# Products of B and input in groups of four tiles, with B rows loaded in each half

## The chip, the core and the metric

The kernel runs on one core of a Trainium2 chip. TensorE (PE) multiplies matrices, VectorE (DVE), ScalarE (ACT) and GpSimd (POOL) work on tiles of 128 partitions, and SyncE (SP) issues transfers between HBM and the on-chip memory. Each engine runs its own list of instructions in order; semaphores tie the lists together. The metric is the device time of one execution in microseconds.

## The reference

The input is 8 batch rows of 512 steps with 128 channels. Four layers with residuals follow each other: a selective state-space layer (S6), a mixture of experts, a diagonal state-space layer (S5), and the same experts again. The part that the change touches is S6, with 256 inner channels and 64 states:

```python
def step(h, t):
    delta_t, B_t, x_t, C_t = t
    dA = jnp.exp(delta_t[..., None] * A)
    dB = delta_t[..., None] * B_t[:, None, :]
    h = dA * h + dB * x_t[..., None]
    y_t = C_t * jnp.sum(h, axis=-1)
    return (h, y_t)
...
x = x + _L0_attn_a_ref(_layernorm(x, axis=-1), ...)
x = x + _L0_ffn_ref(_layernorm(x, axis=-1), ...)
x = x + _L0_attn_b_ref(_layernorm(x, axis=-1), ...)
x = x + _L0_ffn_ref(_layernorm(x, axis=-1), ...)
```

So for each batch row there are 256 x 64 state sequences of 512 steps. Each obeys h = dA * h + w, where w is the product of u = delta * x (one value per channel and step) and B (one value per state and step). The experts (8 of them, all computed and weighted with the routing's weights) and S5 are dense products with short elementwise work between.

## The kernel before

One batch row is one turn of the pipeline, `scan(Turn(...))`; turns count from 0 to 7. A turn has 128 slots, and slot k holds tile k of the scan: 128 partitions (32 groups of channels by 4 groups of states) by 512 steps. `tile_of(k)` gives the half of the channels (k // 64), the state row n (0 to 15) and the channel q (0 to 3) within a group of four. Two tiles make a pair, called a duo in the code.

For each tile ScalarE computes the decay `da` (line 736, an exponential, into PSUM), GpSimd the product `w` = `ur` times `br` (line 845, two tiles in one instruction), VectorE the scan `h` (line 1146), and TensorE sums `h` over states into `ys` (line 569), four tiles at a time. Buffers form rings: `da` holds 4 tiles, `w` 6 tiles (`W_RING` of 3 pairs), `h` 8 tiles. ScalarE and GpSimd therefore run ahead of VectorE by at most 4 and 6 tiles. The pair that may reuse a buffer of `w` is found by `before_in_ring`, which begins anew in every turn: pair 0 takes buffer 0, which pair 63 of the turn before used.

`ur` (input rows u spread over the partitions, two halves of 64 tiles) and `dr` (step rows delta) are loaded from scratch tensors in HBM, where the previous turn stored them. `br` holds all 16 rows of B per partition group; both halves read them. It is loaded once per turn in four chunks of four rows, 1 MB each (line 352, `load_b`), in the turn before and at the start of the turn.

Between the tiles each engine does the other layers' work, at slots that a written table fixes. `weave(pair, tasks)` calls `pair(slot)` and then every task whose slot has come; this is the order in the engine's list, and no engine can pass an instruction that waits. `pre_a` is the preparation of the next batch row (projections, softplus, stores, from slot 64 on), `post` the later layers of the previous row, `late` the last part of the experts of the row before that. GpSimd's tasks are:

- `expert_sums` (line 789): adds the weighted outputs `yk` of an expert to x. It waits for ScalarE (line 697). It stands at slots 6, 13, 18, 24 and 29 (late), 43, 47, 54, 58, 65, 69, 76 and 80 (first experts), 120, 124 and behind 127 (second experts).
- `rstd` (lines 751 to 757): four small instructions of a layer normalization, at slots 13, 22, 70, 83 and 103. ScalarE's normalization and VectorE's statistics (`moments`, line 995) stand on either side.
- `gates` (lines 820 and 823): products for the output gate, at slots 47, 48, 50 and 51, and a residual (line 828) at 54.
- lines 795, 798, 801 and 777: further products of whole rows, at slots 13, 17 and 106 to 107.

VectorE's statistics of the first experts' output stand at slot 77 and wait for the sum of the last expert, which GpSimd has at slot 80. In turn 0 there are no expert tasks at all, and in turn 1 no late ones.

## Time and profile before

| | |
|---|---|
| median of 3 runs | 1941.29 us (1937.05 to 1941.82) |
| span of the profiled execution | 1936.6 us |
| time of the profiled execution around its span | the page gives none |
| VectorE busy | 1522.2 us (79%) |
| GpSimd busy | 1516.6 us (78%) |
| TensorE busy (matmul) | 1377.6 us (71%) |
| ScalarE busy | 1294.2 us (67%) |
| moved by DMA | 88.34 MB, mean 46 GB/s |

The span goes from the first to the last instruction of one execution. Busy time is counted per engine, so the engines' figures do not add up to the span. In the rows further down, "idle before" is the time in which the engine stood still before an instruction, and the arrow names the engine and line whose semaphore came last; "issue" stands where the profile shows no releaser for the wait.

### The profile page before, as it was taken

Reading aid. Unit: us, or ns where it says so; the run is one execution under the profiler, and the core shown is the slowest. Engines: PE = TensorE matmul, PEld = TensorE weight load, DVE = VectorE, ACT = ScalarE, POOL = GpSimd, SP = SyncE. Lnnn points to the kernel's source line nnn. Section 1 sums busy time; section 2 is a strip of 40 time slices with the busy share of each in tenths; the row PEclk is TensorE's granted clock in tenths of the full one; section 3 lists DMA queues with packets and bytes.
Section 4 is the critical chain, followed back from the end, with each engine's and each line's share of the span. In section 5 each row is a group of like instructions: output and inputs, shape, how many; then the busy total and the mean of one; then the engine's idle time right before and its main releaser. Section 6 shows DMA issues by size and latency. Waiting matters only on the chain. (4 is left out here: it accounts for less than half of the span.)

```text
span 1936.6 us, 18983 instructions
## 1 busy us (share of the span) xinstructions
PE 1377.6 (71%) x5928; PEld 611.6 (32%) x5928; DVE 1522.2 (79%) x2109; ACT 1294.2 (67%) x2285; POOL 1516.6 (78%) x888
## 2 busy tenths in 40 slices
PE   3236458777885787768776778668787778668958
PEld 1001113224332343224332343224332343324535
DVE  3979887887888788897888888888878878895222
ACT  4447567677777777677777777777776867665423
POOL 0899899788897798877898798977998888974212
PEclk8557569889897989889898899889898898869969
DMA  3500500031001400031000400032000320000000
GB/s 102 195 0 25 184 1 1 25 109 71 12 1 31 173 12 1 25 109 71 12 1 25 169 11 11 1 103 102 11 1 25 109 71 6 1 6 1 6 1 6
DMA packets 34140, 88.34 MB, mean 46 GB/s; under 512 B 5363, under 2 KB 20598, under 8 KB 25846
## 3 DMA queue, kind: packets, MB, share of 16 engines
q1 hardware_dynamic: 32454, 87.12, 12.7%
q8 instruction: 47, 0.77, 0.2%
q14 instruction: 55, 0.45, 0.1%
q10 hardware_dynamic: 1584, 0.01, 0.0%
HBM read 75.58 MB, written 11.53 MB: 45 GB/s over the span
## 5 line engine op out<-in xcount | busy, mean ns | idle before, releaser
L1146 DVE TENSOR_TENSOR_SCAN h<-da,w 128x512 f32<-128x512 f32 x1024 | 1193.2, 1208 | 225.6 <-ACT da L736 127.5
L845 POOL TENSOR_TENSOR w<-ur,br 128x1024 f32<-128x1024 f32 x512 | 1197.1, 2362 | 158.5 <-DVE h L1146 146.3
L736 ACT ACTIVATE da<-dr,al 128x511 f32<-128x511 f32 x1024 | 683.4, 689 | 236.0 <-DVE h L1146 233.3
L569 PE MATMUL ys<-h,wsum 128*32 128x512 f32 x2048 | 331.8, 726 | 243.2 <-DVE h L1146 215.4
L502 PE MATMUL bankH<-nT,w 128*128 128x512 f32 x512 | 321.3, 713 | 99.8 <-DVE aq L1085 67.9
L789 POOL TENSOR_TENSOR x<-x,yk 128x512 f32<-128x512 f32 x128 | 163.2, 1275 | 193.2 <-ACT yk L697 175.2
L502 PE MATMUL bankG<-nT,w 128*128 128x512 f32 x512 | 292.8, 656 | 25.5 <-DVE aq L1085 25.5
L515 PEld LDWEIGHTS bankY<-w,aq 128*128 128x128 f32 x2048 | 259.2, 200 | 83.7 <-issue 74.1
L515 PE MATMUL bankY<-w,aq 128*128 128x128 f32 x2048 | 265.9, 286 | 9.7 <-DVE aq L1085 5.1
L697 ACT ACTIVATE yk<-bankY,rt 128x128 f32<-128x128 f32 x512 | 156.0, 365 | 132.7 <-PE bankY L515 112.3
L569 PEld LDWEIGHTS ys<-h,wsum 128*32 128x32 f32 x2048 | 43.6, 116 | 446.5 <-DVE h L1146 406.2
L502 PEld LDWEIGHTS bankH<-nT,w 128*128 128x128 f32 x512 | 89.1, 213 | 285.5 <-DVE aq L1085 115.0
L502 PEld LDWEIGHTS bankG<-nT,w 128*128 128x128 f32 x512 | 96.8, 209 | 183.9 <-DVE aq L1085 92.6
L1085 DVE TENSOR_TENSOR aq<-tq,bankH 128x512 f32<-128x512 f32 x64 | 42.8, 669 | 62.0 <-PE bankH L502 62.0
L736 ACT ACT_TABLE_LOAD x62 | 79.5, 1283 | 10.3 <-DMA dr<-d_rows 9.2
L472 PE MATMUL bankG<-xs,wx 128*128 128x512 f32 x64 | 43.7, 819 | 43.1 <-DVE sres L1013 42.3
L684 ACT ACT_TABLE_LOAD x55 | 70.6, 1283 | 1.0
L684 ACT ACTIVATE sq<-bankH 128x512 f32<-128x512 f32 x64 | 38.2, 597 | 46.2 <-PE bankH L502 46.2
L684 ACT ACTIVATE tq<-bankH 128x512 f32<-128x512 f32 x64 | 38.3, 599 | 32.4 <-PE bankH L502 32.1
L631 ACT ACTIVATE nrm<-x,nm,rs 128x128 f32<-128x128 f32 x96 | 39.4, 481 | 29.3 <-POOL nm L757 29.2
L1085 DVE TENSOR_TENSOR aq<-tq,bankG 128x512 f32<-128x512 f32 x64 | 42.6, 666 | 12.5 <-PE bankG L502 12.5
L684 ACT ACTIVATE sq<-bankG 128x512 f32<-128x512 f32 x64 | 38.2, 597 | 20.4 <-PE bankG L502 20.4
(178 smaller groups left out, 1040.4 us busy)
## 6 DMA issues: line engine op xcount, KB each, us to landing
br<-b_rows SPq DMA_DIRECT2D x32, 1024.0 KB, 11.7
dr<-d_rows SPq DMA_DIRECT2D x16, 1024.0 KB, 7.7
ur<-u_rows SPq DMA_DIRECT2D x16, 1024.0 KB, 7.5
d_rows<-vh SPq DMA_DIRECT2D x16, 256.0 KB
u_rows<-th SPq DMA_DIRECT2D x16, 256.0 KB
xnew<-in_L_attn_a_x_dram SPq DMA_DIRECT2D x8, 256.0 KB, 3.0
w<-in_L_ffn_W_dram SPq DMA_DIRECT2D x2, 1024.0 KB, 14.6
x<-in_L_attn_a_x_dram SPq DMA_DIRECT2D x8, 256.0 KB, 9.2
```

Source lines behind the costliest of these rows:

```text
L472: ins = nc.tensor.matmul(p[:, :], lhs(k), xs[:, k, :], start=(k == 0), stop=(k == 1))
L502: is_filled(t, f"{name}{m}_{n}", nc.tensor.matmul(p[:, :], wt[:, n // 2, n % 2 * 128:n % 2 * 128 + 128], nT[:, :], start=True, stop=True))
L515: ins = nc.tensor.matmul(p[:, a * 128:(a + 1) * 128], aq[:, (2 * n + k) % 4, a * 128:(a + 1) * 128], w3[:, n, k, :], start=(k == 0), stop= ...
L569: ins = nc.tensor.matmul(ys[32 * q:32 * q + 32, :], wsum[:, :], h[:, (2 * group + q // 2) % H_RING, q % 2, :], start=(n == 0), stop=(n == ...
L631: A(dst[:, a, :], src[:, a, :], ACT.Identity, bias=nm[:, k, a:a + 1], scale=rs[:, k, a:a + 1]).then_inc(normed[k], 1)
L684: A(zt[j % 4], p[:, :], ACT.Silu).then_inc(drained[BANK[f"h{m}_{j}"]], 1)
L697: ins = A(yk[:, a, :], p[:, a * 128:(a + 1) * 128], ACT.Copy, scale=rt[:, 0, a, e:e + 1])
L736: A(da[duo % D_RING][:, k % 2, 1:L], dr[:, half, q, 1:L], ACT.Exp, scale=nega[:, QUADS * half + q, n:n + 1]).then_inc(decay_ready, 1)
L789: G.tensor_tensor(total[:, :, :], total[:, :, :], yk[:, :, :], ALU.add).then_inc(added, 1)
L845: G.tensor_tensor(w[:, duo % W_RING, :, :], ur[:, half, q:q + 2, :], br[:, n:n + 1, :].to_broadcast([128, 2, L]), ALU.mult).then_inc(produ ...
L1085: drain(f"g{m}_{n}", V.tensor_tensor(aq[:, n % 4, :], zt[n % 4], p[:, :], ALU.mult))
L1146: V.tensor_tensor_scan(h[:, duo % H_RING, k % 2, :], da[duo % D_RING][:, k % 2, :], w[:, duo % W_RING, k % 2, :], 0.0, ALU.mult, ALU.add). ...
```

## The change

- GpSimd multiplies four tiles in one instruction: all four channels q of one state row n, at slots 0, 4, 8 and so on. 256 instructions of 128x2048 replace 512 of 128x1024.
- The ring `w` holds three such groups, twelve tiles, and is indexed by a count that runs on over the turns. `before_in_ring` is gone. A group waits for the scans of the group three before it. `h` is indexed by a running count as well.
- `br` shrinks to two chunks of four rows. Each chunk is loaded anew for each half: 8 chunks per turn, 64 loads of 1 MB instead of 32. A chunk's load waits until the chunk two before it has been multiplied, and is issued by SyncE when its list reaches slots 0, 16, 32 and so on.
- VectorE waits for a product once per four tiles instead of once per two.

```diff
-CHUNKS, PER_CHUNK = 4, 4
+CHUNKS, PER_CHUNK, B_RING = 8, 4, 2
+PER_LOAD = PAIRS // CHUNKS
...
-        w = sb("w", [128, W_RING, 2, L]); h = sb("h", [128, H_RING, 2, L])
+        w = sb("w", [128, W_RING, QUADS, L]); h = sb("h", [128, H_RING, 2, L])
...
+                i, n0 = chunk // CHUNKS, chunk % CHUNKS * PER_CHUNK % PER_QUAD
                 sp.wait_ge(b_stored, 16 * i + 16)
-                if not known(i, 1):
-                    sp.wait_ge(product_ready, DUOS * (i - 1) + DUO_HALF + 2 * PER_CHUNK * (chunk + 1))
...
+                if not known(chunk, B_RING):
+                    sp.wait_ge(product_ready, PER_CHUNK * (chunk - B_RING + 1))
...
             def scan(t):
                 def pair(k):
+                    if k % PER_LOAD == 0 and not (k == 0 and known(t.b, 1)) and (t.pre or k < PAIRS - PER_LOAD):
+                        load_b(CHUNKS * t.b + k // PER_LOAD + 1)
                     if k == 0 and not known(t.b, 1):
-                        load_b(t.b, CHUNKS - 1)
                         load_steps(t.b, 1)
...
-                    if k % 2:
+                    if k % QUADS:
                         return
...
-                    freed = before_in_ring(duo, W_RING)
-                    if not known(DUOS * t.b + freed, 0):
-                        pool.wait_ge(scanned, PAIRS * t.b + 2 * freed + 2)
-                    G.tensor_tensor(w[:, duo % W_RING, :, :], ur[:, half, q:q + 2, :],
-                                            br[:, n:n + 1, :].to_broadcast([128, 2, L]), ALU.mult).then_inc(product_ready, 1)
+                    chunk, quad = (PAIRS * t.b + k) // PER_LOAD, DUO_HALF * t.b + k // QUADS
+                    if k % PER_LOAD == 0:
+                        pool.wait_ge(b_in[chunk % B_RING], 16 * (chunk // B_RING) + 16)
+                    if not known(quad, W_RING):
+                        pool.wait_ge(scanned, QUADS * (quad - W_RING) + QUADS)
+                    row = n % PER_CHUNK
+                    G.tensor_tensor(w[:, quad % W_RING, :, :], ur[:, half, :, :],
+                                    br[:, chunk % B_RING, row:row + 1, :].to_broadcast([128, QUADS, L]), ALU.mult).then_inc(product_ready, 1)
...
+                    quad = DUO_HALF * t.b + k // QUADS
+                    if k % QUADS == 0:
+                        v.wait_ge(product_ready, quad + 1)
                     if k % 2 == 0:
-                        v.wait_ge(product_ready, DUOS * t.b + duo + 1)
```

GpSimd's list from slot 44 to slot 64, before (w is the product, x the expert sum, cg, xd and resa the gates and the residual):

```order
L845 TENSOR_TENSOR w<-ur,br 128x1024 [waits scanned] x2
L820 TENSOR_TENSOR cg<-cm,sres 128x512 [waits c_ready,ys_taken]
L789 TENSOR_TENSOR x<-x,yk 128x512 [waits added,drainedY,weighted]
L845 TENSOR_TENSOR w<-ur,br 128x1024 [waits scanned,b_in3]
L823 TENSOR_TENSOR xd<-xd,sres 128x512 [waits skip_ready]
L845 TENSOR_TENSOR w<-ur,br 128x1024 [waits scanned]
L820 TENSOR_TENSOR cg<-cm,sres 128x512
L823 TENSOR_TENSOR xd<-xd,sres 128x512 [waits skip_ready]
L845 TENSOR_TENSOR w<-ur,br 128x1024 [waits scanned] x2
L828 TENSOR_TENSOR resa<-xn,bcs 128x512 [waits normed0,x1_ready]
L789 TENSOR_TENSOR x<-x,yk 128x512 [waits added,drainedY,weighted]
```

The same place now:

```order
L842 TENSOR_TENSOR w<-ur,br 128x2048 [waits scanned]
L817 TENSOR_TENSOR cg<-cm,sres 128x512 [waits c_ready,ys_taken]
L786 TENSOR_TENSOR x<-x,yk 128x512 [waits added,drainedY,weighted]
L842 TENSOR_TENSOR w<-ur,br 128x2048 [waits scanned,b_in1]
L820 TENSOR_TENSOR xd<-xd,sres 128x512 [waits skip_ready]
L817 TENSOR_TENSOR cg<-cm,sres 128x512
L820 TENSOR_TENSOR xd<-xd,sres 128x512 [waits skip_ready]
L842 TENSOR_TENSOR w<-ur,br 128x2048 [waits scanned]
L825 TENSOR_TENSOR resa<-xn,bcs 128x512 [waits normed0,x1_ready]
L786 TENSOR_TENSOR x<-x,yk 128x512 [waits added,drainedY,weighted]
```

The products of tiles 50 and 51 have moved ahead of the gates at slots 48, 50 and 51.

GpSimd's list around a turn's start (slot 116 to slot 7), before; b_in0 and input_in0 mark the product of tile 0:

```order
L845 TENSOR_TENSOR w<-ur,br 128x1024 [waits scanned] x7
L789 TENSOR_TENSOR x<-x,yk 128x512 [waits drainedY,weighted]
L845 TENSOR_TENSOR w<-ur,br 128x1024 [waits scanned] x2
L789 TENSOR_TENSOR x<-x,yk 128x512 [waits added,drainedY,weighted]
L845 TENSOR_TENSOR w<-ur,br 128x1024 [waits scanned]
L789 TENSOR_TENSOR x<-x,yk 128x512 [waits added,drainedY,weighted]
L845 TENSOR_TENSOR w<-ur,br 128x1024 [waits scanned,b_in0,input_in0]
```

And now:

```order
L842 TENSOR_TENSOR w<-ur,br 128x2048 [waits scanned] x2
L786 TENSOR_TENSOR x<-x,yk 128x512 [waits drainedY,weighted]
L842 TENSOR_TENSOR w<-ur,br 128x2048 [waits scanned]
L786 TENSOR_TENSOR x<-x,yk 128x512 [waits added,drainedY,weighted] x2
L842 TENSOR_TENSOR w<-ur,br 128x2048 [waits scanned,b_in0,input_in0]
```

The last products of a turn (tiles 126 and 127) have moved ahead of the sum at slot 124, and two sums now stand directly in front of tile 0.

SyncE's list for the end of one turn and the start of the next, before (br is the load of B rows, dr and ur those of step and input rows, d_rows and u_rows the stores):

```order
L352 DMA br<-b_rows 128x1x2048 [waits product_ready,b_stored]
L319 DMA d_rows<-vh 4x32x512 [waits drainedG]
L325 DMA u_rows<-th 4x32x512 [waits inputs_ready]
L330 DMA dr<-d_rows 128x1x2048 [waits decay_ready,steps_stored0]
L330 DMA ur<-u_rows 128x1x2048 [waits product_ready,inputs_stored0]
L319 DMA d_rows<-vh 4x32x512 [waits drainedH]
L325 DMA u_rows<-th 4x32x512 [waits inputs_ready]
L352 DMA br<-b_rows 128x1x2048 [waits product_ready,b_stored] x3
L330 DMA dr<-d_rows 128x1x2048 [waits decay_ready,steps_stored1]
L330 DMA ur<-u_rows 128x1x2048 [waits product_ready,inputs_stored1]
```

And now:

```order
L349 DMA br<-b_rows 128x1x2048 [waits product_ready,b_stored]
L315 DMA d_rows<-vh 4x32x512 [waits drainedG]
L321 DMA u_rows<-th 4x32x512 [waits inputs_ready]
L326 DMA dr<-d_rows 128x1x2048 [waits decay_ready,steps_stored0]
L326 DMA ur<-u_rows 128x1x2048 [waits product_ready,inputs_stored0]
L315 DMA d_rows<-vh 4x32x512 [waits drainedH]
L321 DMA u_rows<-th 4x32x512 [waits inputs_ready]
L349 DMA br<-b_rows 128x1x2048 [waits product_ready,b_stored] x2
L326 DMA dr<-d_rows 128x1x2048 [waits decay_ready,steps_stored1]
L326 DMA ur<-u_rows 128x1x2048 [waits product_ready,inputs_stored1]
```

The load of a turn's first B chunk stood in the first of these rows and now stands in the eighth, behind both stores and both loads; the first row is now the last chunk of the running turn.

## Rows read from the trace of the kernel before

**Rows 1.** Costliest groups: line, engine, out<-in, shapes, count | busy us, mean ns | idle before us.

```profile
L845 POOL TENSOR_TENSOR w<-ur,br 128x1024 f32<-128x1024 f32 x512 | 1197.1, 2362 | 158.5 <-DVE h L1146 146.3
```

**Rows 2.** Waits: engine and line, what it waited for: us in total, times, longest.

```profile
POOL x L789 <- ACT yk L697: 175.2, 53, 17.5
POOL w L845 <- DVE h L1146: 146.3, 102, 5.9
DVE h L1146 <- issue: 52.9, 26, 3.0
DVE h L1146 <- POOL w L845: 3.2, 1, 3.2
```

**Rows 3.** Windows: stretch, us, busy us (and instructions) of PE, PEld, DVE, ACT, POOL; clock, DMA.

```profile
114.00:145.00 31.00, 7.82 (x36) 0.89 (x40) 19.48 (x18) 11.43 (x18) 31.00 (x18) 0.50 0.00 0
...
830.00:1040.00 210.00, 160.38 (x714) 73.17 (x713) 176.16 (x239) 155.64 (x275) 181.97 (x108) 0.88 0.13 45
```

**Rows 4.** Timeline, GpSimd at turn 4's start: start us, length, instruction xcount [idle before <-releaser].

```profile
884.22 1.27 POOL L789 TENSOR_TENSOR x<-x,yk 128x512 f32<-128x512 f32 x1 [1.37 <-ACT yk L697]
887.77 9.30 POOL L845 TENSOR_TENSOR w<-ur,br 128x1024 f32<-128x1024 f32 x4 [2.28 <-DVE h L1146]
```

**Rows 5.** Timeline, VectorE, turn 4's start (tiles 127 and 0) and tile 26.

```profile
886.38 1.22 DVE L1146 TENSOR_TENSOR_SCAN h<-da,w 128x512 f32<-128x512 f32 x1
890.22 2.34 DVE L1146 TENSOR_TENSOR_SCAN h<-da,w 128x512 f32<-128x512 f32 x2 [2.62 <-issue]
...
936.90 4.65 DVE L1146 TENSOR_TENSOR_SCAN h<-da,w 128x512 f32<-128x512 f32 x4 [1.20 <-issue]
```

**Rows 6.** Timeline, GpSimd, turn 4, from the sum before tile 48 to tile 61.

```profile
969.29 1.27 POOL L789 TENSOR_TENSOR x<-x,yk 128x512 f32<-128x512 f32 x1 [2.44 <-DVE h L1146]
970.51 2.36 POOL L845 TENSOR_TENSOR w<-ur,br 128x1024 f32<-128x1024 f32 x1
...
991.76 6.97 POOL L845 TENSOR_TENSOR w<-ur,br 128x1024 f32<-128x1024 f32 x3
```

**Rows 7.** Timeline, VectorE, the same stretch (first row: tiles 45 to 48; then 52, 56, 60).

```profile
969.73 4.56 DVE L1146 TENSOR_TENSOR_SCAN h<-da,w 128x512 f32<-128x512 f32 x4
...
981.27 3.54 DVE L1146 TENSOR_TENSOR_SCAN h<-da,w 128x512 f32<-128x512 f32 x3 [2.42 <-issue]
...
988.36 4.66 DVE L1146 TENSOR_TENSOR_SCAN h<-da,w 128x512 f32<-128x512 f32 x4 [1.26 <-issue]
...
994.21 1.22 DVE L1146 TENSOR_TENSOR_SCAN h<-da,w 128x512 f32<-128x512 f32 x1 [0.61 <-ACT da L736]
```

**Rows 8.** Timeline, GpSimd, turn 4, slots 69 to 80.

```profile
1006.82 1.27 POOL L789 TENSOR_TENSOR x<-x,yk 128x512 f32<-128x512 f32 x1 [2.25 <-ACT yk L697]
...
1010.35 0.20 POOL L751 TENSOR_TENSOR var<-bag,eps 128x4 f32<-128x4 f32 x1
...
1012.16 7.00 POOL L845 TENSOR_TENSOR w<-ur,br 128x1024 f32<-128x1024 f32 x3
...
1024.99 1.26 POOL L789 TENSOR_TENSOR x<-x,yk 128x512 f32<-128x512 f32 x1
```

**Rows 9.** Timeline, VectorE, turn 4, the statistics at slot 77.

```profile
1026.29 0.87 DVE L995 BATCH_NORM_STATS2 bst<-x 128x6 f32<-128x128 f32 x4 [2.08 <-POOL x L789]
```

**Rows 10.** Timeline, GpSimd, turn 0, tiles 6 to 47.

```profile
63.48 48.53 POOL L845 TENSOR_TENSOR w<-ur,br 128x1024 f32<-128x1024 f32 x21 [5.94 <-DVE h L1146]
```

**Rows 11.** Timeline, VectorE, turn 0 tile 71, turn 1 tiles 0 and 14.

```profile
155.81 4.57 DVE L1146 TENSOR_TENSOR_SCAN h<-da,w 128x512 f32<-128x512 f32 x4 [1.30 <-ACT da L736]
...
232.15 2.34 DVE L1146 TENSOR_TENSOR_SCAN h<-da,w 128x512 f32<-128x512 f32 x2 [2.61 <-issue]
...
251.35 3.53 DVE L1146 TENSOR_TENSOR_SCAN h<-da,w 128x512 f32<-128x512 f32 x3 [1.00 <-ACT da L736]
```

**Rows 12.** The tile br: from a DMA's issue to its landing.

```profile
DMA to landing us min/median/max: 4.8/11.7/15.7
```

More of the change, by code:

```diff
@@ L111, in tile_of @@
     return k // HALF, (k % HALF) // QUADS, k % QUADS
-def before_in_ring(duo, ring):
-    return duo - ring if duo >= ring else max(d for d in range(DUOS) if d % ring == duo % ring) - DUOS
 def moe_pe(m, late):
@@ L245, in hybrid_kernel @@
         delta_in = [sem("delta_in0"), sem("delta_in1")]; input_in = [sem("input_in0"), sem("input_in1")]
-        b_in = [sem(f"b_in{c}") for c in range(CHUNKS)]
+        b_in = [sem(f"b_in{c}") for c in range(B_RING)]
         decay_ready = sem("decay_ready"); product_ready = sem("product_ready")
@@ L363, in pre_a @@
                 store_b(t)
-                yield HALF + 18
-                load_b(i, 0)
+                if first:
+                    yield HALF + 18
+                    load_b(0)
                 yield SLOT["dt1"] + 10
@@ L374, in pre_a @@
                 store_inputs(t, 1)
-                for chunk in range(1, CHUNKS - 1):
-                    yield HALF + 18 + 16 * chunk
-                    load_b(i, chunk)
                 if first:
-                    load_b(i, CHUNKS - 1)
+                    yield HALF + 34
+                    load_b(1)
                     load_steps(i, 1)
@@ L568, in sum_states @@
                     for q in range(QUADS):
-                        ins = nc.tensor.matmul(ys[32 * q:32 * q + 32, :], wsum[:, :], h[:, (2 * group + q // 2) % H_RING, q % 2, :],
+                        ins = nc.tensor.matmul(ys[32 * q:32 * q + 32, :], wsum[:, :], h[:, (DUOS * t.b + 2 * group + q // 2) % H_RING, q % 2, :],
                                                start=(n == 0), stop=(n == PER_QUAD - 1))
@@ L831, in pair @@
                 def pair(k):
-                    if k % 2:
+                    if k % QUADS:
                         return
-                    half, n, q = tile_of(k)
-                    duo = k // 2
+                    half, n, _ = tile_of(k)
                     if k == 0 and known(t.b, 1):
```

19 lines of the change are left out of this document (9 added, 10 removed).

## The prediction

> **What bounds the kernel now.** Five views were read, in this order. The costliest groups of instructions show GpSimd's products of the reference's B and input term: 512 instructions of two tiles each, 2362 ns [rows 1]. A tile is one 128x512 piece of state, 128 of them in a turn (one batch row). The table of waits looks as if these products never mattered: VectorE's scans waited for them 3.2 us in all, and GpSimd waited 146.3 us for the scans and 175.2 us for ScalarE's weighted expert outputs [rows 2]. But 52.9 us of scan idle are put down to "issue", and the order of time explains that name: in one of the middle turns scans start at 890.22, 936.90, 981.27, 988.36 and 994.21, each after a gap [rows 5, 7], and the product they read ends about 0.1 us before. For the first, the product started at 887.77 and takes 2.36 us, so it ended at 890.13 [rows 4]. The windows say the same: from 114 to 145 us GpSimd was busy in all 31.00 us, VectorE in 19.48. In a middle window of 210 us neither is full, 182 and 176 us [rows 3]. So no engine bounds this kernel as a whole. The engines run written orders and hand the lateness round, and what decides is who is late at each place. I count five places per turn where GpSimd is: tile 0 (gap 2.62), 26 (1.20), 52 (2.42), 56 (1.26) and 60 (0.61), 8.1 us together [rows 5, 7]. In the first turn it is more. Turns are numbered from 0, so this one is turn 4.
>
> **What one product of four tiles costs.** No row shows a GpSimd instruction of 2048 columns. Starts tell more than lengths here: 21 two-tile products cover 48.53 us [rows 10], so (48.53 - 2.36)/20 = 2.31 us from one to the next, and the one-tile instruction at 969.29 is followed at 970.51, 1.22 us [rows 6]. A further tile costs 2.31 - 1.22 = 1.09, the fixed part is 0.13. Bounds: 4 x 1.09 = 4.36 with no fixed part at all, 4 x 1.22 = 4.88 with the whole of it each time. I take 1.22 + 3 x 1.09 = 4.49, nearest to both rows, against 4.62 for two of today's: 0.13 us saved per four tiles, 256 x 0.13 = 33 us of GpSimd over the run. Its end is seen 0.05 later (2.36 against 2.31).
> By the rows, a product's span is 2.36 us and its spacing 2.31. The Trainium skill (Perfetto Trace Analysis, section GPSIMD Engine Instruction) says that a span reported for GpSimd is not to be trusted and that starts of consecutive instructions should be used; the trace agrees, by 0.05 us. Going by spans one would have 2.36 + 2 x 1.09 = 4.54 and a saving of 0.18, or 46 us; on the path computed below this changes the time by under 3 us.
>
> **The ring.** The old ring held three pairs, six tiles, and began again in each turn: since 64 pairs are not a multiple of 3, pair 0 took the buffer of pair 63 and had to wait for the last scan. The new one holds twelve tiles and runs on across turns.
> At a middle turn's start: the last expert sum starts at 884.22 and ends GpSimd's work at 885.5; then it waits 2.28 us for the scan that ends at 887.60 [rows 4, 5]. Without that wait the four-tile product runs 885.45 to 889.99, and scan 0 can start at 890.1 instead of 890.22. The wait goes, and the longer instruction takes its place: gain 0.1 us, not 2.6. The sum itself cannot come earlier, since it waits for ScalarE, which follows the scans.
>
> **Tiles 24 to 31.** Before tile 14 GpSimd stood waiting for ScalarE (the sum behind tile 12, see the order); products 14 and 15 now fill that wait. From there to tile 29 eight products of 2.31 (18.5 us) become four of 4.49 (18.0), with the same small work between: the gap at tile 26 [rows 5] goes, a smaller one appears before tile 28, which waits for its whole four. I count 0.3 us gained.
>
> **Tiles 48 to 63: the place that costs.** The sum in front of product 48 starts at 969.29 whatever the ring [rows 6]; its row names a scan, but by the order it can only wait for ScalarE's outputs, which ScalarE gives in step with the scans. Today products of 48-49, 50-51 and so on follow with a gate instruction (1.22 us) between them, and scan 48 starts at 969.73 + 3 x 1.12 = 973.1 [rows 7]. After the change the first product is whole only at 970.51 + 4.54 = 975.05: scan 48 starts 2.0 us later. Then three gate instructions (3.66): second product from 978.66, whole at 983.2, scan 52 at 983.3 against 981.27, +2.0. Then two (2.44): scan 56 at 990.2 against 988.36, +1.8. Then one (1.22): scan 60 at 995.9 against 994.21, +1.7. GpSimd has no less to do before tile 63 than before, and the scans get nothing until four tiles are ready. With the 0.3 from above: +1.4 us at tile 60. All of the expert work behind (TensorE's products wait for VectorE's gating in between) moves with it.
>
> **Tiles 69 to 80.** The sum at 1006.82 waits for ScalarE [rows 8], so it moves by 1.4 too. From its start to the end of the last sum (1024.99 + 1.26 = 1026.25) it is 19.43 us today. After: sum 1.22, the four small normalization instructions 1.81 (1010.35 to 1012.16), two products 8.98, sum 1.22, product 4.49, sum 1.26 = 18.98. VectorE stands at exactly this end, 2.08 us until 1026.29 [rows 9]: it is later by 1.4 - 0.45 = 0.9 us. Behind it, products have 4 to 7 us to spare and nothing of GpSimd's decides until the next turn. So a middle turn becomes 0.9 us longer. Six of the eight (turns 2 to 7): +5.4 us.
>
> **First two turns.** Here no expert sums hold GpSimd back, and the ring's size works. It waited 5.94 us for a scan after three products [rows 10]; with twelve tiles allowed it arrives at the gates about 6.0 us earlier than at 112.0. Nine two-tile products up to tile 64 (20.8 us) become five of four (22.4): 1.6 back, so scan 64 comes 4.5 us earlier. The normalization behind it, for which the scans waited 1.30 us [rows 11], also comes earlier: 5.5. At the second turn's start the gap of 2.61 us goes fully, as no sum stands in front; with 0.7 of small gaps in the 20 tiles before, and the gap of 1.00 at tile 14 [rows 11], 4.3 more. Against that the second turn pays the 48 to 80 stretch, +0.9. Together -5.5 - 4.3 + 0.9 = -8.9 us.
>
> **B rows.** Each half reads them anew: 64 loads of 1 MB instead of 32, through SyncE's queue. A load lands in 11.7 us in the middle, 15.7 at worst [rows 12], and a chunk is four products, at least 4 x 4.49 = 18 us. It is asked for when the chunk before last is consumed, so one chunk of work covers it, and I cost it at nothing. The cover is thinnest for a turn's first chunk, behind two stores and two loads of 1 MB: in the first turn it should land about when it is needed. What waits behind a late B load on SyncE are the next turn's step and input rows, needed half a turn later. Without the cover each chunk would lose what it is late by.
>
> **Sum.** -8.9 + 5.4 = -3.5 us. The page gives the profiled execution's span, 1936.6 us, and no other time of it; the median of the runs is 1941.3, 4.7 above, which I take as what lies around it and the spread. Forecast 1941.3 - 3.5 = 1938 us. Unknown sizes: product 4.36 to 4.88 moves a middle turn by -0.8 to +2.3; early gain 5 to 11. That puts the likeliest case between 1932 and 1945.
>
> **Rivals.**
> *The twelve-tile lead works everywhere.* For it: GpSimd waited 146.3 us for scans [rows 2], all of it lead that it could not build. If the gaps at tiles 0 and 26 go in all turns (3.8 x 7 = 27 us, less 5 that I have counted already), the time is 1938 - 22 = 1916. Against it: the 175.2 us behind ScalarE cap the lead in front of tiles 0 and 48.
> *First tile late.* The slower end: the two extra tiles in front of scan 48 (+2.0) and in front of the sum at tile 80 are paid in full, as nothing is won back between tile 60 and 80. Price 2.0 x 7 = 14, early gain 5.5: 1941.3 + 8.5 = 1950. It decides from about 1.4 us per turn upward. For it: TensorE's and ScalarE's gaps at 64, 84 and 108 hang on scans too. Against: the sum of 18.98 against 19.43.
> *B late.* If the first chunk of each turn came 5 us late, 7 x 5 = 35: 1976. Against it: [rows 12].
> *No fixed part is saved.* Then four tiles cost 4.62, a middle turn +1.5: 1942.
>
> **Chances.** Forecast's own case 0.60, lead works 0.16, first tile late 0.18, B late 0.03, nothing saved 0.03. About 0.3%, 6 us, is what a measurement can tell from no change. Of the forecast's 0.60, 0.16 lie under 1935.5, 0.40 within, 0.04 above 1947. Faster 0.16 + 0.16 = 0.32; same 0.40 + 0.03 = 0.43; slower 0.04 + 0.18 + 0.03 = 0.25. The range leaves out the far half of the first rival and the last one: 1921 to 1951.
>
> **What would show it.** Products near 4.5 us, 256 of them. Scan 0 of turn 1 about 9 us earlier, later turns each 0.5 to 1.5 us longer than before; gaps of about 2 us before tiles 48, 52 and of 1.3 before 56; the wait in front of the sum-bound statistics at tile 77 still there. Waits of GpSimd's products for scans nearly gone, for ScalarE's outputs grown. A product that waits for a B load, or middle turns shorter than before, would prove me wrong.

## The result and the profile after

The kernel after took 1952.01 us (median of 4 runs, 1950.81 to 1955.07) against 1941.05 before: ratio 1.0066, 95% interval 1.0051 to 1.0080. It is slower, by 0.7%. The forecast was 1938, and the time lies just outside the range that ended at 1951. The profiled execution took 1950.81 us for a span of 1949.0, so 1.8 us lie around the span (I had taken 4.7 for it and the spread).

What was forecast of the instruction itself came. One row answers [rows 1]:

```profile
L842 POOL TENSOR_TENSOR w<-ur,br 128x2048 f32<-128x2048 f32 x256 | 1154.9, 4529 | 70.7 <-DVE h L1146 58.0 <-issue 12.6
```

256 products of 4.53 us, 4.48 from start to start (885.80, 9.00 us for two, below); GpSimd is busy 1478.2 us instead of 1516.6. The products' waits for scans fell from 146.3 to 58.0, and the expert sums' waits for ScalarE rose from 175.2 to 234.5 [rows 2]:

```profile
POOL x L786 <- ACT yk L694: 234.5, 60, 18.8
```

B rows are loaded 64 times, landing in 4.5 us at least, 5.0 median, 12.3 at most (before [rows 12]), and no product waited for one.

The turn's start, GpSimd and VectorE, against [rows 4, 5]: the product follows the last sum at once, and scan 0 is late as before.

```profile
884.57 1.26 POOL L786 TENSOR_TENSOR x<-x,yk 128x512 f32<-128x512 f32 x1 [3.68 <-DVE h L1146]
885.80 9.00 POOL L842 TENSOR_TENSOR w<-ur,br 128x2048 f32<-128x2048 f32 x2
```

```profile
890.40 2.34 DVE L1146 TENSOR_TENSOR_SCAN h<-da,w 128x512 f32<-128x512 f32 x2 [2.45 <-issue]
...
973.64 1.22 DVE L1146 TENSOR_TENSOR_SCAN h<-da,w 128x512 f32<-128x512 f32 x1 [1.97 <-issue]
...
981.78 2.34 DVE L1146 TENSOR_TENSOR_SCAN h<-da,w 128x512 f32<-128x512 f32 x2 [2.38 <-issue]
985.71 1.22 DVE L1146 TENSOR_TENSOR_SCAN h<-da,w 128x512 f32<-128x512 f32 x1 [1.59 <-ACT da L733]
...
996.16 3.44 DVE L1146 TENSOR_TENSOR_SCAN h<-da,w 128x512 f32<-128x512 f32 x3
1004.11 1.22 DVE L1146 TENSOR_TENSOR_SCAN h<-da,w 128x512 f32<-128x512 f32 x1 [4.50 <-PE ys L566]
...
1028.09 0.87 DVE L992 BATCH_NORM_STATS2 bst<-x 128x6 f32<-128x128 f32 x4 [1.79 <-POOL x L786]
```

The rows at 973.64 and 981.78 are scans 48 and 52: gaps of 1.97 and 2.38, as worked out for the place that costs [rows 7]. Both scans start only 0.5 us later than before (973.1 and 981.27), since 1.5 us had been gained at tile 32, of which the forecast knew nothing. The gap of 1.3 us forecast in front of scan 56 is not there; instead scan 54 waits 1.59 us for its decay (row at 985.71). The wait at the statistics of slot 77 is still there [rows 9]. So far most steps hold. Two things were not in my sum. The first is the start. Before, VectorE's last setup instructions:

```profile
50.51 0.15 DVE L975 TENSOR_TENSOR s5w<-s5w 128x1 f32<-128x1 f32 x1
50.58 2.34 DVE L976 SCALAR_TENSOR_TENSOR s5w<-s5w 128x1 f32<-128x1 f32 x1
52.95 2.40 DVE L978 SCALAR_TENSOR_TENSOR cosT<-cosT,s5w,rT 128x128 f32<-128x128 f32 x1
55.27 2.42 DVE L979 SCALAR_TENSOR_TENSOR sinT<-sinT,s5w,tq 128x128 f32<-128x128 f32 x1
```

After, VectorE and then GpSimd:

```profile
51.06 4.62 DVE L976 SCALAR_TENSOR_TENSOR sinT<-sinT,s5w,tq 128x128 f32<-128x128 f32 x1
55.60 4.45 DVE L977 SCALAR_TENSOR_TENSOR s5w<-s5w 128x1 f32<-128x1 f32 x1
60.08 4.55 DVE L970 TENSOR_SCALAR rT<-sinT,s5w 128x256 f32<-128x256 f32 x1
64.55 0.34 DVE L971 TENSOR_SCALAR tq<-cosT,s5w 128x256 f32<-128x256 f32 x1
...
67.49 3.45 DVE L1146 TENSOR_TENSOR_SCAN h<-da,w 128x512 f32<-128x512 f32 x3 [0.22 <-DVE mc L984]
```

```profile
51.03 13.45 POOL L842 TENSOR_TENSOR w<-ur,br 128x2048 f32<-128x2048 f32 x3 [12.62 <-issue]
```

Instructions that take 0.15 to 0.35 us elsewhere in the setup (one on 128x1!) take about as long as one product each, three of 2.3 to 2.4 before and three of 4.5 to 4.6 after. Scan 0 starts at 67.49 instead of 61.06.

The second is TensorE. Two places of turn 4 show it. The first is the experts' tile 8 at slot 50: its matmuls wait until VectorE has done a gating product `aq` behind scan 49. Before, then after:

```profile
974.93 1.12 PE L502 MATMUL bankH<-nT,w 128*128 128x512 f32 x2 [0.63 <-DVE aq L1085]
976.64 1.12 PE L502 MATMUL bankG<-nT,w 128*128 128x512 f32 x2 [0.59 <-DVE aq L1085]
```

```profile
975.50 1.25 PE L499 MATMUL bankH<-nT,w 128*128 128x512 f32 x2 [2.71 <-DVE aq L1082]
977.21 2.07 PE L499 MATMUL bankG<-nT,w 128*128 128x512 f32 x2 [0.46 <-DVE aq L1082]
```

TensorE stood still 2.71 us in one piece, and then a pair of matmuls takes 2.07 instead of 1.12: it runs at 1.2 instead of 2.4 GHz. The windows (columns as in [rows 3], the clock stands behind GpSimd's time) have that stretch first, granted clock 1.00 before and 0.53 after, and then whole turns from scan 0 to scan 0. Before, then after:

```profile
976.00:983.00 7.00, 5.49 (x23) 2.99 (x23) 4.58 (x6) 5.91 (x8) 7.00 (x5) 1.00 0.00 0
...
890.20:1112.10 221.90, 168.61 (x741) 75.58 (x740) 186.45 (x250) 163.16 (x287) 188.83 (x111) 0.88 0.14 48
```

```profile
976.00:983.00 7.00, 6.54 (x9) 2.13 (x8) 4.62 (x6) 3.90 (x6) 7.00 (x5) 0.53 0.00 1
...
667.30:890.40 223.10, 170.61 (x741) 76.72 (x740) 186.50 (x249) 163.06 (x287) 184.09 (x79) 0.87 0.19 66
890.40:1114.20 223.80, 171.71 (x742) 76.89 (x741) 186.55 (x250) 162.98 (x287) 184.03 (x79) 0.87 0.18 66
1114.20:1340.90 226.70, 174.04 (x740) 78.62 (x739) 186.47 (x249) 162.98 (x287) 184.01 (x79) 0.86 0.18 65
```

VectorE's and ScalarE's work is the same to 0.3 us, GpSimd has 4.8 us less, and the turn's length goes with TensorE's busy time: 168.6 in 221.9 us, 170.6 in 223.1, 171.7 in 223.8, 174.0 in 226.7. TensorE does no more matmuls; more of them fall into stretches at 1.2 GHz.

The second place is scan 64, and it is where turn 4 gets its extra length. Scans 61 to 63 start at 996.16 (row above), before at 995.93: up to there the kernel after is level, to 0.2 us. Scan 64 waits for TensorE's sums `ys` of the tiles before it, and starts 1.9 us later than before. VectorE and TensorE before:

```profile
995.93 3.45 DVE L1146 TENSOR_TENSOR_SCAN h<-da,w 128x512 f32<-128x512 f32 x3
1002.22 1.22 DVE L1146 TENSOR_TENSOR_SCAN h<-da,w 128x512 f32<-128x512 f32 x1 [2.85 <-PE ys L569]
```

```profile
1000.99 1.07 PE L569 MATMUL ys<-h,wsum 128*32 128x512 f32 x8
```

And TensorE after:

```profile
1002.12 1.81 PE L566 MATMUL ys<-h,wsum 128*32 128x512 f32 x8
```

The wait grew from 2.85 to 4.50 us, and the same eight matmuls take 1.81 instead of 1.07 us. Which of the two places costs the time, the experiments tell.

### The profile page after: what moved, and what is told of

Read it like the earlier page. It is cut to its first block, busy times and chain, and to the rows that moved or that the text cites. A ratio compares the mean times of both kernels' runs of the same rounds, so it can differ in the third digit from the quotient of the medians.

```text
span 1949.0 us, 18801 instructions
## 1 busy us (share of the span) xinstructions
PE 1398.8 (72%) x5928; PEld 619.3 (32%) x5928; DVE 1526.6 (78%) x2109; ACT 1292.9 (66%) x2285; POOL 1478.2 (76%) x632
## 3 DMA queue, kind: packets, MB, share of 16 engines
q1 hardware_dynamic: 37062, 120.67, 17.4%
## 4 chain that ended last, share of the span: by engine, by line
PE 29%; DVE 22%; POOL 21%; ACT 15%; issue 11%; SPq 1%; DVEq 0%; POOLq 0%; DMA 0%; ACTq 0%
POOL w L842 16%; DVE h L1146 14%; PE bankH L499 8%; PE bankG L499 7%; ACT da L733 5%; PE bankY L512 4%; PE ys L566 3%; DVE aq L1082 3%; POOL x L786 3%; ACT L733 3%; PE bankG L469 2%; ACT yk L694 2%; ACT L681 2%; PE bankY L493 1%; DVE bst L992 1%
## 5 line engine op out<-in xcount | busy, mean ns | idle before, releaser
L842 POOL TENSOR_TENSOR w<-ur,br 128x2048 f32<-128x2048 f32 x256 | 1154.9, 4529 | 70.7 <-DVE h L1146 58.0
L499 PE MATMUL bankH<-nT,w 128*128 128x512 f32 x512 | 325.7, 722 | 101.4 <-DVE aq L1082 72.5
L786 POOL TENSOR_TENSOR x<-x,yk 128x512 f32<-128x512 f32 x128 | 162.9, 1273 | 284.5 <-ACT yk L694 234.5
L499 PE MATMUL bankG<-nT,w 128*128 128x512 f32 x512 | 306.1, 683 | 28.4 <-DVE aq L1082 28.4
L512 PEld LDWEIGHTS bankY<-w,aq 128*128 128x128 f32 x2048 | 263.5, 203 | 88.9 <-issue 80.7
L512 PE MATMUL bankY<-w,aq 128*128 128x128 f32 x2048 | 270.2, 288 | 9.7 <-DVE aq L1082 5.2
L748 POOL TENSOR_TENSOR var<-bag,eps 128x4 f32<-128x4 f32 x40 | 8.3, 207 | 71.4 <-DVE bag L995 71.4
```

What stands on the lines that cost most here:

```text
L499: is_filled(t, f"{name}{m}_{n}", nc.tensor.matmul(p[:, :], wt[:, n // 2, n % 2 * 128:n % 2 * 128 + 128], nT[:, :], start=True, stop=True))
L512: ins = nc.tensor.matmul(p[:, a * 128:(a + 1) * 128], aq[:, (2 * n + k) % 4, a * 128:(a + 1) * 128], w3[:, n, k, :], start=(k == 0), stop= ...
L786: G.tensor_tensor(total[:, :, :], total[:, :, :], yk[:, :, :], ALU.add).then_inc(added, 1)
L842: G.tensor_tensor(w[:, quad % W_RING, :, :], ur[:, half, :, :], br[:, chunk % B_RING, row:row + 1, :].to_broadcast([128, QUADS, L]), ALU.m ...
```

## The experiments

All were compared with the kernel before on the same chip (1938 to 1939 us there; 1941.05 for the result above, whose 1952.0 stands in the row `after`). One table gives what the traces show, one profiled execution each; starts are those of scan 0 of turns 1 and 2 and of the last scan (tile 127 of turn 7), in us.

| kernel | turn 1 | turn 2 | lengths of turns 2 to 6 | last scan | median us | ratio |
|---|---|---|---|---|---|---|
| before | 232.1 | 446.5 | 222.2 221.5 221.9 221.9 222.0 | 1766.8 | 1939 | 1 |
| after | 231.4 | 441.8 | 225.5 223.1 223.8 226.7 223.8 | 1780.1 | 1952.0 | 1.0066 |
| after_again | 235.2 | 450.0 | 222.0 223.7 223.3 223.8 226.7 | 1779.7 | 1951.1 | 1.0059 |
| e1_start | 226.5 | 439.9 | 223.9 223.2 221.8 221.9 221.8 | 1762.6 | 1948.7 | 1.0036 |
| e2_pairs | 228.3 | 435.9 | 222.1 221.5 221.9 221.9 221.9 | 1758.2 | 1932.2 | 0.9968 |
| e4_mix | 232.4 | 444.1 | 222.1 225.1 221.9 221.9 221.9 | 1767.4 | 1938.2 | 0.9998 |
| g3_pairs_48_51 | 231.1 | 442.9 | 225.6 221.6 223.3 221.8 221.9 | 1767.6 | 1937.0 | 0.9983 |
| h2_pairs_48_51_calm_start | 226.6 | 438.4 | 223.5 225.1 221.8 221.9 221.9 | 1763.1 | 1933.0 | 0.9972 |
| g1_before_late_48 | 233.1 | 448.0 | 227.9 222.7 225.4 223.7 223.3 | 1787.4 | 1956.6 | 1.0087 |
| g2_before_late_0 | 235.4 | 450.8 | 222.2 221.5 221.9 221.9 222.0 | 1769.6 | 1938.1 | 0.9994 |
| e6_before_running_ring | 231.6 | 442.9 | 222.2 221.5 221.9 221.9 222.0 | 1765.5 | 1937.0 | 0.9989 |
| e8_pairs_calm_start | 227.7 | 437.4 | 222.2 221.5 221.9 221.9 222.0 | 1759.7 | 1930.1 | 0.9948 |
| h1_before_calm_start | 231.4 | 445.9 | 222.2 221.5 221.9 221.9 222.0 | 1766.1 | 1936.8 | 0.9996 |
| e5_pairs_ring6 | 230.6 | 442.4 | 222.2 221.5 221.9 221.9 222.0 | 1764.8 | 1936.5 | 0.9988 |
| f1_after_filled | 233.2 | 443.7 | 228.5 225.5 226.7 221.8 221.9 | 1778.2 | 1947.7 | 1.0048 |
| f2_before_filled | 232.9 | 447.6 | 222.3 223.5 219.9 223.8 220.0 | 1766.9 | 1937.5 | 0.9994 |
| f3_best_filled | 226.7 | 437.5 | 225.6 221.6 221.9 225.2 218.8 | 1768.6 | 1938.7 | 0.9992 |

### The start (e1_start, h1_before_calm_start)

```diff
+                    if k == 4 and known(t.b, 1):
+                        pool.wait_ge(drained["Y"], 1)
```

Expected:

> Only change against the changed kernel: in the first turn the second product (tiles 4 to 7) waits until VectorE has finished its setup tables. Theory P (a VectorE instruction with two operands in SBUF stands still while a GpSimd product reads SBUF): VectorE's setup instructions take 0.2 to 0.5 us again except about one, and the first scan starts near 59 us instead of 67.5. GpSimd starts its second product 4 us later than before, so what the scans gain GpSimd's lead loses; scan 0 of turn 1 within 3 us of 231.4 and the whole 1947 to 1953 us. Rival (the setup is late because of transfers or something else): the setup instructions stay at 4.5 us and the first scan at 67.5.

Measured: median 1948.7 us, ratio 1.0036 (1.0016 to 1.0056); ten runs, eight from 1944.9 to 1950.5, one at 1939.6 and the profiled one at 1932.0, so the trace is that of the fastest execution. VectorE's setup now stands beside one product only, and scan 0 starts at 58.89:

```profile
50.78 4.47 DVE L977 SCALAR_TENSOR_TENSOR cosT<-cosT,s5w,rT 128x128 f32<-128x128 f32 x1
55.17 0.34 DVE L978 SCALAR_TENSOR_TENSOR sinT<-sinT,s5w,tq 128x128 f32<-128x128 f32 x1
...
58.89 3.45 DVE L1148 TENSOR_TENSOR_SCAN h<-da,w 128x512 f32<-128x512 f32 x3 [0.22 <-DVE mc L986]
```

The hold is shown: move the products away and it goes. Of 8.6 us at scan 0, 4.9 are left at turn 1, more than the 3 that were expected at most.

More telling is that one program took 1932 and 1950 us. In the profiled execution turns 4 to 6 are 221.8 to 221.9 us long with four-tile products throughout, as long as before. At slot 50 nothing is better than in the kernel after: TensorE stands still just as long and its matmuls slow down just as much.

```profile
972.03 1.18 PE L499 MATMUL bankH<-nT,w 128*128 128x512 f32 x2 [2.69 <-DVE aq L1084]
973.75 2.08 PE L499 MATMUL bankG<-nT,w 128*128 128x512 f32 x2 [0.53 <-DVE aq L1084]
```

So the fall of the clock behind slot 50 does not by itself make a turn longer. The two executions part later, at the experts' tile 12 (slot 61). The kernel after, then e1_start:

```profile
994.34 1.13 PE L499 MATMUL bankH<-nT,w 128*128 128x512 f32 x2 [1.73 <-DVE aq L1082]
996.30 1.57 PE L499 MATMUL bankG<-nT,w 128*128 128x512 f32 x2 [0.83 <-DVE aq L1082]
998.41 2.08 PE L499 MATMUL bankH<-nT,w 128*128 128x512 f32 x2 [0.54 <-ACT tq L681]
```

```profile
990.87 1.12 PE L499 MATMUL bankH<-nT,w 128*128 128x512 f32 x2 [1.73 <-DVE aq L1084]
992.86 1.13 PE L499 MATMUL bankG<-nT,w 128*128 128x512 f32 x2 [0.86 <-DVE aq L1084]
994.97 1.13 PE L499 MATMUL bankH<-nT,w 128*128 128x512 f32 x2 [0.99 <-ACT tq L681]
...
996.88 1.06 PE L566 MATMUL ys<-h,wsum 128*32 128x512 f32 x8
```

From 60 to 106 us behind scan 0 of turn 4 every matmul of the two starts at the same distance from scan 0, to 0.04 us, and the standstills are the same. Then the clock falls in one and stays up in the other. The windows from 100 to 112 us behind scan 0 (before, after, e1_start):

```profile
990.20:1002.20 12.00, 8.45 (x20) 2.49 (x19) 8.56 (x9) 8.01 (x15) 12.00 (x7) 0.72 0.01 2
```

```profile
990.40:1002.40 12.00, 8.89 (x29) 3.75 (x32) 9.05 (x9) 7.56 (x14) 12.00 (x4) 0.77 0.22 87
```

```profile
987.00:999.00 12.00, 8.43 (x37) 3.83 (x36) 9.87 (x10) 9.30 (x16) 12.00 (x4) 1.00 0.25 89
...
1108.80:1330.70 221.90, 169.62 (x741) 77.11 (x740) 186.46 (x250) 163.04 (x287) 183.93 (x79) 0.88 0.18 66
```

```profile
998.11 1.22 DVE L1148 TENSOR_TENSOR_SCAN h<-da,w 128x512 f32<-128x512 f32 x1 [1.95 <-PE ys L566]
```

Between the two kernels with four-tile products, scan 64 waits 4.50 us for TensorE's sums with the clock at 0.77 in this stretch (row at 1004.11 above) and 1.95 with 1.00 (row at 998.11). That is 2.55 us from the clock alone, in one turn, in the same instructions; 2.0 of them are left in the turn's length (223.8 against 221.8). But the mean of the stretch does not tell it: before it is lower still, 0.72, and scan 64 waits only 2.85. What matters is whether the low stretch lies over the sums. Granted clock by the distance behind scan 0, with the wait of scan 64 and the turn's length:

| turn | 86 to 93 us | 103 to 106 | 107 to 110 | 110 to 113 | scan 64 waits | turn |
|---|---|---|---|---|---|---|
| before, 4 | 1.00 | 0.50 | 0.53 | 1.00 | 2.85 | 221.9 |
| after, 4 | 0.52 | 1.00 | 0.50 | 0.50 | 4.50 | 223.8 |
| e1_start, 4 | 0.51 | 1.00 | 1.00 | 1.00 | 1.95 | 221.8 |
| f1_after_filled, 4 | 1.00 | 1.00 | 1.00 | 0.73 | 3.55 | 226.7 |
| f1_after_filled, 5 | 1.00 | 1.00 | 1.00 | 1.00 | 1.95 | 221.8 |
| g3_pairs_48_51, 5 | 1.00 | 1.00 | 0.53 | 1.00 | 2.77 | 221.8 |

Why the clock fell at 106 us in one execution and not in the other, behind the same standstills, no run shows.

Expected of the calm start in the kernel before (the same two lines with `k == 2`):

> The kernel before, the second product of turn 0 held until VectorE's setup is done. Before, three setup instructions stand 2.3 to 2.4 us each beside three products, 7.0 us in all. If their hold is real and nothing swallows it, scan 0 comes at 55 to 57 instead of 61.1 us and the time is 1939 - 5 = 1934. If turn 0 swallows it, because the six-tile ring makes GpSimd wait for scans and ScalarE for VectorE anyway, scan 0 is earlier but turn 1 starts as before: 1939.

Measured: 1936.8 us, 0.9996 (0.9987 to 1.0005). This lies between the two expectations. Scan 0 comes at 57.7 instead of 61.1, but turn 0 swallows most of it: the lead is 3.4 us at tile 0, 1.3 at tile 60 and 0.7 when turn 1 starts. What does it was not tested.

### Size of the product (e2_pairs, e4_mix, g3_pairs_48_51)

```diff
+def by_pairs(b, k):
+    return 48 <= k < 64
...
-                    G.tensor_tensor(w[:, quad % W_RING, :, :], ur[:, half, :, :],
+                    G.tensor_tensor(w[:, quad % W_RING, q:q + size, :], ur[:, half, q:q + size, :],
```

Ring, running count and B loads stay those of after. e2_pairs has pairs everywhere:

> The changed kernel with products of two tiles again; ring of twelve tiles that runs on over the turns and B loaded in each half are kept. Theory G (the size of the group costs: no scan can start before all four tiles are ready): scan 48 of a middle turn comes 2.0 us earlier relative to the turn's start than in the changed kernel, scan 0 of a turn comes 2.3 us earlier than in the kernel before, the gap at tile 26 goes; per middle turn about 3 us less than before and 6 less than changed, whole 1915 to 1930 us. Rival B (the second loading of B costs): at least 1945. Rival R (the longer lead and the ring's new order cost): at least 1945.

e4_mix has them in slots 48 to 63:

> The changed kernel with products of two tiles in slots 48 to 63 only, four everywhere else. Theory G: scan 48 comes 2.0 us earlier in each turn and most of that stays, 1952 - 14 = 1938 us (1934 to 1943). Rival (the time went elsewhere: TensorE's clock, the statistics behind tile 77, B loads): 1948 to 1952.

g3_pairs_48_51 in slots 48 to 51:

> The kernel after, with products by two tiles in slots 48 to 51 only. Pairs in slots 48 to 63 gave 1938. Place theory: the first group behind the sum (scan 48 +2.0 us) is what makes TensorE stand still 2.7 us at slot 50 and lets its clock fall at 86 us; without it 1938 to 1943. If scans 52, 56 and 60 matter as much, it stays at 1947 to 1951.

Measured: 1932.2 (0.9954 to 0.9982), 1938.2 (0.9989 to 1.0007) and 1937.0 (0.9975 to 0.9992). e2 is above its 1915 to 1930: its middle turns are as long as before, since the ring's lead gained nothing there. One group out of 32, the first behind the sum, carries 1951 - 1937 = 14 us; splitting the next three too adds nothing. In g3 (the trace is that of its slowest execution, 1938.3 us) the gating of tile 8 is in time and the clock stays up at slot 50, while scan 52 is as late as in the kernel after (981.78 there):

```profile
974.97 1.12 PE L519 MATMUL bankG<-nT,w 128*128 128x512 f32 x2 [0.59 <-DVE aq L1104]
```

```profile
981.75 3.45 DVE L1168 TENSOR_TENSOR_SCAN h<-da,w 128x512 f32<-128x512 f32 x3 [4.59 <-ACT da L753]
```

The late scans from 52 on are therefore not what costs. Nor does the clock at slot 50 settle it: it is up in all middle turns of g3, and two of them are still long (225.6 and 223.3), with the clock low again between 104.5 and 111.3 us behind scan 0.

### Lateness alone, put into the kernel before (g1_before_late_48, g2_before_late_0)

```diff
+                    if k == 48 and not known(t.b, 1):
+                        for n_spare in range(2 * (t.b - 1), 2 * t.b):
...
+                            G.tensor_tensor(spare[:, :], ur[:, half, q, 0:496], br[:, n, 0:496], ALU.mult).then_inc(spare_done, 1)
```

> The kernel before, with two further GpSimd products of 496 columns into a spare tile in front of the product of tiles 48 and 49, in turns 1 to 7 (about 2.4 us, as much as the larger group delays scan 48 in the kernel after). Nothing else of the change is in it. If the place 48 to 63 costs what a step in my sum said (the delay reaches the statistics at slot 77, less nothing), each middle turn gets 1.5 to 2.4 us longer: 1939 + 7 x 2 = 1953. If a delay there only counts when it changes where TensorE's granted clock falls, turns are 221.9 us as before or 223 to 227 us, and nothing between: 1939 to 1955.

> The kernel before, with one further GpSimd product of 496 columns (about 1.2 us) in front of the product of tile 0, in turns 1 to 7. Sum of waits: scan 0 waits for that product already (gap 2.6 us), so each turn gets 1.2 us longer, 1939 + 8 = 1947. Theory that the turn's length is tied to where the clock falls: either 221.9 us as before, since a turn has 1 to 2 us of play there (the running ring saved 2.3 us at this place and turns kept 221.9), so 1939 to 1941, or a step to 223 us and more in some turns.

Measured: 1956.6 us (1.0073 to 1.0100) and 1938.1 us (0.9984 to 1.0003). With none of the change in it, 2.4 us of GpSimd in front of tile 48 give the picture of after in the middle turns: scan 48 late by 2.4, TensorE still for 3.03 us, matmul pairs at 2.03 to 2.08, turns of 222.7 to 227.9. The expectation that no turn lies between 221.9 and 223 was missed by one turn (222.7), and the time is above both expectations. By its size alone this time could also be a plain shift, 7 x 2.4 = 17 us; against a shift that is always paid stand the turns of 221.8 us with a late scan 48 in e1_start and f1_after_filled.

```profile
985.63 2.08 PE L502 MATMUL bankH<-nT,w 128*128 128x512 f32 x2 [3.03 <-DVE aq L1090]
```

In front of tile 0, 1.2 us vanish. Scan 0 waits 3.86 instead of 2.62, and by tile 4 each turn is back on its old course:

```profile
894.48 2.34 DVE L1151 TENSOR_TENSOR_SCAN h<-da,w 128x512 f32<-128x512 f32 x2 [3.86 <-issue]
```

So 1.2 us more in front of tile 0 change no middle turn, and 2.4 us more in front of tile 48 make one longer by 2.7 us on average.

### Ring and B loads (e6_before_running_ring, e5_pairs_ring6)

```diff
-                    freed = before_in_ring(duo, W_RING)
-                    if not known(DUOS * t.b + freed, 0):
-                        pool.wait_ge(scanned, PAIRS * t.b + 2 * freed + 2)
+                    turn_duo = DUOS * t.b + duo
+                    if not known(turn_duo, W_RING):
+                        pool.wait_ge(scanned, 2 * (turn_duo - W_RING) + 2)
```

> The kernel before with one edit: its ring of three pairs runs on over the turns, so that the first product of a turn does not wait for the last scan. Theory G: scan 0 comes 2.3 us earlier in each of seven turns and that stays, 1941 - 16 = 1925 us (1921 to 1930). Rival: the time is given back at tiles 4 and 14, where the scans wait for ScalarE's decays: 1938 to 1942.

> Products by two tiles, a running ring of six tiles, B loaded in each half. The kernel before with the running ring (1937.0) differs from it only in where B comes from; the one with a ring of twelve (1932.2) only in the ring. B costs nothing, as forecast: 1937.0 within 1 us. If the doubled transfers or the wait for a chunk cost, it is above 1940.

Measured: 1937.0 (0.9980 to 0.9998) and 1936.5 (0.9979 to 0.9997). The two differ only in where B comes from, and by 0.5 us (ratios 0.9989 and 0.9988): B costs nothing. The running ring takes 2.3 us of the gap at tile 0 of turn 4 away and moves no middle turn:

```profile
886.67 2.34 DVE L1146 TENSOR_TENSOR_SCAN h<-da,w 128x512 f32<-128x512 f32 x2 [0.28 <-issue]
```

Twelve instead of six tiles (e2 against e5) are worth 4.3 us in the medians; in the traces they are worth 6.5 us when turn 2 starts, and nothing more behind it.

### TensorE kept busy (f1_after_filled, f2_before_filled, f3_best_filled)

```diff
+            def keep_busy(n):
+                for _ in range(n):
+                    nc.tensor.matmul(ys[0:32, :], ident[0:64, 64:96], w1[0:64, 0:2, :].rearrange("p e h -> p (e h)"),
+                                     start=False, stop=False)
...
+                        if name == "h" and m == 1 and n in (8, 12) and t.b < NB:
+                            keep_busy(3)
```

> The kernel after, and TensorE multiplies by zeros three times (128x512, added to the sums) in front of the first experts' tile 8 (slot 50) and tile 12 (slot 61) in turns 1 to 7. In the kernel after TensorE stands still 2.7 us and 1.7 to 2.2 us there, and its granted clock is at the lower level from 86 and from 104 us behind scan 0 in every middle turn. If the clock is what makes the middle turns long (223.1 to 226.7 us), these two low stretches go or shrink, the middle turns come back to about 222 and the time is about 1949 - 14 = 1935. If GpSimd's late groups alone make them long, nothing is given back and the multiplications cost up to 1 us a turn: 1950 to 1957.

> The kernel before with the same multiplications by zeros at the same two places. TensorE stands still there 0.9 us and 3.2 us. Clock theory: its low stretch from 103 us goes; the turn of 221.9 us is held by the other low stretches, so 1935 to 1942. Rival: three more instructions (some 2 us) in front of tile 8 cost 1 us a turn where only 0.9 us was idle: 1946.

> Products by two tiles with ring of twelve tiles and calm start (1930.1 us), and TensorE multiplies by zeros in turns 1 to 7 in front of what it waits for: 3 times at slot 22, 4 at 61, 7 at 81, 2 at 92, 6 at 102, about 0.7 us each where it stands still 2.3, 3.4, 6.8, 2.3 and 5.3 us. If the turn's length hangs on the clock's low stretches (51 us a turn now), these shrink to 20 us or less and the turn falls below 221.9, to some 218: 1930 - 7 x 4 = 1902 to 1920. If it hangs on GpSimd, VectorE and ScalarE alone, it stays 221.9 or grows by what the multiplications overrun: 1930 to 1940.

Measured: 1947.7 (1.0035 to 1.0061), 1937.5 (0.9985 to 1.0003) and 1938.7 us (0.9983 to 1.0001). f1 misses its number. The low stretch at slot 50 went in all middle turns, but in turns 2 to 4 the clock was still low around 108 to 115 us behind scan 0, and these took 225.5 to 228.5 us. In turns 5 and 6 both stretches were gone, and they took 221.8 and 221.9, no less than the turns of e1_start in which the clock falls at slot 50. The fall at slot 50 is thus neither enough for a long turn nor needed for one. f2 has its time as expected, but not its turns: they change between 219.9 and 223.8 us, 221.9 on average. f3 lies within the second of its two expectations by its time, not by its turns: the granted clock rose to 0.90 and more, and turns 4 to 6 took 221.9, 225.2 and 218.8.

```profile
1106.50:1331.70 225.20, 189.25 (x788) 80.60 (x784) 186.69 (x250) 163.16 (x288) 188.33 (x111) 0.90 0.18 66
1331.70:1550.50 218.80, 180.47 (x788) 78.27 (x784) 186.36 (x249) 162.92 (x288) 188.39 (x111) 0.95 0.19 67
```

So not the mean clock decides but where it is low. Filling TensorE's idle time, as done here, gives nothing back; whether the multiplications make their own lateness was not tested.

### One value or several (after_again), both causes away (h2_pairs_48_51_calm_start), the best (e8_pairs_calm_start)

> The kernel after unchanged, to see whether its time has more than one value, as the variant with a calm start had (1932 to 1950). Clock theory: most runs 1948 to 1955, now and then one that falls in step earlier, 1940 or below. Rival (late groups alone): one value, 1951 within 0.2%.

Measured: 1949.1 to 1951.6 in five runs, none near 1940. But its turns 2 to 6 are not those of the first trace, turn by turn, and one of them is 222.0. The time has one value in these runs, the way there differs.

> The kernel after with both causes taken away: products by two tiles in slots 48 to 51 (1937.0 alone) and the second product of turn 0 held until VectorE's setup is done (scan 0 at 58.9 instead of 67.5 us, 5 us earlier at the start of turn 1). If these two are the whole loss: 1937 - 5 = 1932, turns of 221.9 us from turn 2 or 3 on. If something else of the change still costs: 1937 or more.

Measured: 1933.0 (1931.7 to 1934.0), ratio 0.9972 (0.9961 to 0.9983). With both causes removed the changed kernel is 5 us faster than before, near the forecast's -3.5. Turns 2 and 3 of its trace are still long (223.5 and 225.1, expected 221.9 from turn 2 or 3 on), so the two causes carry the loss of 11 us, but not every long turn is gone.

> Products by two tiles, ring of twelve tiles that runs on, B loaded in each half, and the second product of turn 0 waits until VectorE's setup is done. Both theories: scan 0 comes at about 59 instead of 67.4 us, and the ring's lead stays: 1932 - 5 = 1927 if the turns keep their length of 221.9 us, not below 1922. If the start's 8 us are swallowed by turn 0's ring as 4 of them were in the variant with four-tile products, 1929 to 1932.

Measured: 1930.1 us, ratio 0.9948 (0.9935 to 0.9961): it beats both kernels. It keeps ring and B loads of the change, with products of two tiles, and the calm start (`k == 2`). The expectation of 1929 to 1932 came, by which turn 0 swallows the earlier start: turn 1 starts 0.6 us earlier than in e2_pairs (1932.2, 0.9954 to 0.9982). The two intervals overlap, so that the calm start is worth anything here is not shown.

## Why the prediction was wrong

Point by point.

- Product of four tiles, 4.49 from start to start: right (4.48). Wait at the turn's start replaced by the longer instruction: right (scan 0 at 890.40, forecast 890.1). B at no cost: right (e5 against e6). Tile 48 late by 2.0: right as a step (the shift grows from -1.5 to +0.5 us at tile 48 in turn 4).
- First two turns, -8.9: missed a term. Turn 1 starts 0.7 us earlier (forecast about 9) and turn 2 4.7 (forecast 8.9). With the start's hold away (h2) turn 1 starts 5.5 and turn 2 8.1 us earlier, so the term at nothing was the hold, 6.4 us at scan 0. That h2 comes near 8.9 is in part luck: scan 64 of turn 0 is 2.1 us earlier in it (forecast 4.5), and turn 1 wins more than forecast. The trace of before had the rows: three setup instructions of 2.3 to 2.4 us stood beside the first three products. The Trainium skill (SBUF — State Buffer, section SBUF: two separate sides) says that VectorE and GpSimd share a pair of ports, which is locked for a whole instruction, and that a VectorE instruction with two SBUF inputs, or in a fast mode of two ports, needs it. The trace agrees (4.62, 4.45 and 4.55 beside products of 4.53). The scans, 1.2 us each whatever GpSimd does, read one of their inputs from PSUM.
- **Middle turn +0.9, six of them +5.4: this step failed.** From the start of turn 2 to the last scan the kernel after loses 18.0 us (from -4.7 to +13.3). The delay at tile 48 was as forecast. What failed is the line "all of the expert work behind moves with it": I let the delay pass through TensorE as a shift, kept TensorE's durations as they were, and priced everything behind tile 63 by GpSimd's gaps alone. In turn 4 nothing but 0.2 us is lost up to scan 63; 1.7 us are lost at scan 64, which waits 4.50 instead of 2.85 us for TensorE's sums, since the granted clock is 0.50 over most of them. Where it was 1.00 there (e1_start, turns 4 to 6), the late tile 48 cost nothing at all, 221.8 us, less than my +0.9. Where it was not, turns took 223.1 to 226.7. g3 shows that 14 us hang on the group of tile 48 alone, g1 that lateness there is enough without the rest of the change. The Trainium skill (TensorE: Matmul & The Clock Gate, section HAM oscillation — how this bites in real kernels) says that waits between groups of matmuls can drop the clock each time anew. The trace agrees for slot 50: 2.71 us without work, and pairs of matmuls at 2.07 instead of 1.12. But that fall cost nothing, and the one at slot 61 that did cost came behind 1.73 and 0.83 us in the kernel after and not behind 1.73 and 0.86 in e1_start. How a late tile 48 brings the low stretch over the sums of scan 64 therefore stays open.
- The rivals. "First tile late" (1950) had place and price right, 2.0 x 7 = 14 us, and the slower end, and it named gaps at 64 and 108; that it is paid there through TensorE's clock, and in some turns not at all, was not in it, so the price is in part luck. "The lead works everywhere" is refuted by e6 and g2: 2.3 us less or 1.2 more in front of tile 0 change no middle turn. "B late" and "nothing saved" did not happen.
- Tiles 24 to 31, forecast 0.3: the trace of turn 4 shows 0.3 by tile 28 and 1.8 by tile 32. In turns 5 and 7 of the same trace the 1.5 of it are missing.
- The 8.1 us of GpSimd's gaps that I counted per turn were no measure of anything. Removing the largest (tile 0, e6) moved no middle turn, and lengthening the one at tile 48 by a pure delay cost 17.4 us (g1).

Why the middle turns of so many kernels take the same 221.9 us, whatever is saved in front of tile 0, stays open. In these kernels the low stretches of TensorE's clock lie at the same distance from scan 0 turn after turn, and in the kernel after they wander from turn to turn. Turns with the same low stretches have the same length in the traces, to 0.2 us, but turns of 221.8 us come with several patterns (table above); that the pattern of the clock holds the length, rather than the length the pattern, was not shown.
